# Gathers of the first two chunks with all fields of three examples, and their pair tiles picked by TensorE

## The chip, the cores and the metric

The kernel runs on one core of one Trainium2 chip. The metric is the device time in microseconds (us) of the whole program; lower is better. Before the change three runs took 1071.68, 1075.14 and 1076.42 us, median 1075.14. One further execution was recorded by the hardware profiler; all rows of the trace come from it. TensorE multiplies matrices, VectorE, ScalarE and GpSimd work on tiles in SBUF (on chip) and in PSUM (eight banks of 128 x 512 float32, where TensorE writes), and SyncE only starts transfers.

## What is computed

A compressed interaction network over 39 embedding fields of 16 elements, for 512 examples, and a small network behind it:

```python
e = jnp.stack([tbl_0[ids[:, 0]], ..., tbl_38[ids[:, 38]]], axis=1)     # (512, 39, 16): x
...
for k in range(3):                                                     # 128 units each
    z = jnp.einsum('bmd,bhd->bdmh', x, prev).reshape(b, D, m * h)
    t = jnp.einsum('bdc,co->bdo', z, ws[k]) + bs[k]
    t = jnp.transpose(t, (0, 2, 1))
    t = t / jnp.sqrt(jnp.sum(t * t, axis=(-2, -1), keepdims=True))
    logit.append(t)
    prev = t
# the sums over d of the three t, and dense_ctx: 400 features into layers of 512, 256 and 1
```

In layer 0 prev is x itself, so its products are pairs of fields; in layers 1 and 2 they are 39 fields by 128 units. All in float32.

## The kernel before

The batch is cut into 16 chunks of 32 examples. A chunk has 32 x 16 = 512 columns (example, element).

**From tables to pairs.** For each chunk GpSimd gathers rows by ten indirect DMAs (`gather`, L390), the 39 x 32 rows of field and example, 128 at a time and 96 in the last. SyncE stores them to `x_scratch` in device memory (`store_chunk`, L467 to L471) and loads them back with fields on partitions (`load_reps`, `load_partners`, helper L333): the field itself, repeated three times over 117 partitions plus 11 extra rows (`x_reps`), and its partners 2 to 19 fields on, in six tiles (`x_rot`). VectorE multiplies both (`make_pairs`, L896) into `z0`, in groups of two tiles that wait for `pairs_loaded[0]`, `[1]`, `[2]`; ScalarE makes the squares (`square_x`), VectorE their low part (L880). TensorE sums tiles 0 to 5 with folded weights (`pair_matmul`, L754, float32) and the squares (L752) into `acc0`: layer 0 before bias and norm. For chunk 0 three of the tiles aren't loaded but picked by TensorE out of 39 rows (`pick`, L771).

**Jobs.** Layers 1 and 2 are done in 128 jobs of 128 columns: `JOBS` has jobs 0 to 3 for layer 1 of chunk 0, then in turns four of layer 1 of a chunk and four of layer 2 of the one before. A job computes, for each field, weights times prev into a bank of four fields, by three float32r matmuls of split operands (`three_terms`, L686 to L688). Ten banks: five for ScalarE (`bank_a`, a ring of two), five for VectorE (`bank_d`, a ring of three), in turns D, A, D, A (places 0 to 9). ScalarE scales its banks by x (L531), GpSimd adds them (L407); VectorE scales and adds its 20 fields (u = 0 to 19) one by one (`add_field`, L918). ScalarE's banks are made seven ahead (`LEAD`), so before job 0 there are seven of them. `turn_sums` (L727) transposes the sum of job n - 1 at place 5 of job n.

**What sets the order.** Each engine's program is one list in a fixed order, with waits on semaphores; nothing is reordered. Tables of numbers say at which (job, place) or (job, field) other work stands in it: `PAIRS_AT` for VectorE's `make_pairs` of chunk c, `PAIR_MATMULS_AT` for the sums, `W2_HIGH_AT` and `W2_LOW_AT` for the split of layer 2's weights, `FINISHES` and `NORMS` for bias, sums and norm. In GpSimd's program `gather(it + 2, ...)` stands behind the adds a = 1, 2, ... of a job of round it. GpSimd's adds in job n's turn belong to bank 5n + 7 + a.

**The start.** GpSimd gathers chunks 0 and 1 and seven of chunk 2's ten before its first add. TensorE waits for chunk 0's gathers and keeps busy with matmuls whose results nobody reads (`keep_busy`, L777). ScalarE rounds the weights of layer 1 (`split_high`), VectorE takes the rest (`split_low`, L870). Chunk 1's pairs are made by VectorE before job 0 and summed by TensorE inside job 0.

Of the kernel before, what the change touches and what calls it, by code (L numbers as in the profile page):

```python
# [5 lines left out]
FIELDS = 39  # L6
# [107 lines left out]
for _c in range(1, CHUNKS):  # L114
    _it = _c - 1
    if _it == 0:

        _made = []
        _summed = {(0, 0): [0, 1], (0, 2): [2, 3], (0, 4): [4, 5], (0, 6): [6]}
    else:  # L120
        _first = (step_at(_it, 0), 2) if _it == 1 else (step_at(_it - 1, 7), 12)
        _made = [_first, (step_at(_it, 0), 12), (step_at(_it, 1), 12 if _it > 1 else 17), (step_at(_it, 2), 5)]
# [3 lines left out]
    if _it:  # L126
        SQUARES_AT[step_at(_it, 1), 3] = _c
# [10 lines left out]
GATHERS_BEFORE = 7  # L138
# [18 lines left out]
def cin_kernel(nc, idx_in, base_in, table, ctx_t, w0a, w0b, w1, w2, b0, b1, b2,  # L157
# [7 lines left out]
    with ExitStack() as ctx:  # L165
# [8 lines left out]

        ids_sb = sb("ids_sb", [128, CHUNKS * GATHERS], i32)
# [39 lines left out]
        twice = scaled[0:FIELDS, 0, 0, 0:2 * FIELDS]  # L215
        turns = scaled[0:FIELDS, 1, 0:PICKED, :]
# [32 lines left out]

        ids_loaded = sem("ids_loaded")  # L250
# [57 lines left out]

        NOT_LOADED = [PER_TILE + 2, 1, 0, 0]
# [68 lines left out]
        def _(pool):  # L378
# [4 lines left out]
            def start_chunk(c):  # L383
                if c >= 2:
# [756 lines left out]
```

## Time and profile before

| | |
|---|---|
| runs, us | 1071.68, 1075.14, 1076.42 (median 1075.14) |
| profiled execution | 1074.81 us, its span in the trace 1073.1 us |
| TensorE matmul | 1039.9 us busy, 97% of the span |
| VectorE | 970.8 us, 90% |
| GpSimd | 864.2 us, 81% |
| ScalarE | 797.3 us, 74% |
| chain that ended last | TensorE 66%, GpSimd 18%, VectorE 8%, issue 5% |

PE is TensorE's matmul unit, PEld its weight load, DVE is VectorE, ACT ScalarE, POOL GpSimd, SP SyncE; a q behind a name is that engine's sequencer, which issues DMAs. Times count from the span's start. A float32 matmul is recorded twice, so x12 in a row of L777 or L754 is six instructions; a float32r matmul once. The busy time of a matmul is modelled with its end, so the distance between starts is the better price. "idle before" is the engine's idle time ahead of an instruction, with what ended it.

### The profile page before, as it was taken

To read this page: it belongs to the slowest core of one execution; us is meant where nothing else is said; L and a number is where in the kernel's file an instruction comes from. 1 tells how busy PE (TensorE), PEld (TensorE's weight loads), DVE (VectorE), ACT (ScalarE), POOL (GpSimd) and SP (SyncE) were. 2 spreads that over 40 slices of the span, in tenths; PEclk is the share of its full clock that TensorE was granted. 3 is DMA by queue.
4 is the path that set the end of the run, shared out by engine and by line. 5 is a ranking of instruction groups with operands and counts; after the bars stand their busy time and mean duration, and the time that the engine had idled before them with its cause. 6 is when DMAs were issued, how large, how long until landed. Compare 5 with 4: busy or idle time off the path is not lost.

```text
span 1073.1 us, 18076 instructions
## 1 busy us (share of the span) xinstructions
PE 1039.9 (97%) x4386; PEld 790.4 (74%) x4386; DVE 970.8 (90%) x3326; ACT 797.3 (74%) x2670; POOL 864.2 (81%) x729
## 2 busy tenths in 40 slices
PE   2999999999999999999999999999999999999998
PEld 0466777878777787877778787777878777788783
DVE  2489999999999999999999999999999999999893
ACT  3476777868788786878778787877878787788772
POOL 6677888988888898888889888888988888586670
PEclk9999999999999999999999999999999999999999
DMA  5531030301403030120303012030301203000000
GB/s 189 140 100 23 3 83 3 84 2 16 125 3 82 3 83 2 28 58 3 83 3 83 1 34 52 3 83 3 84 2 24 61 3 82 1 1 1 1 1 1
DMA packets 59381, 44.02 MB, mean 41 GB/s; under 512 B 39177, under 2 KB 42121, under 8 KB 59146
## 3 DMA queue, kind: packets, MB, share of 16 engines
q1 hardware_dynamic: 51975, 36.49, 13.8%
q0 software_dynamic: 5120, 1.29, 1.4%
q10 hardware_dynamic: 2179, 5.07, 1.4%
q8 instruction: 35, 0.57, 0.2%
q14 instruction: 72, 0.59, 0.2%
HBM read 40.89 MB, written 1.94 MB: 40 GB/s over the span
## 4 chain that ended last, share of the span: by engine, by line
PE 66%; POOL 18%; DVE 8%; issue 5%; ACT 3%; DMA 1%; POOLq 0%; SPq 0%; DVEq 0%; ACTq 0%
POOL sums L407 13%; PE bank_a L686 10%; PE bank_d L686 9%; PE bank_d L688 9%; PE bank_d L687 9%; PE bank_a L688 9%; PE bank_a L687 9%; PE acc L754 7%; POOL gathered L390 4%; DVE sums L918 4%; ACT scaled L531 1%; PE turned L777 1%; ACT sums L531 1%; PE turned L727 1%; PE bank_d L855 1%
## 5 line engine op out<-in xcount | busy, mean ns | idle before, releaser
L407 POOL TENSOR_TENSOR sums<-sums,scaled 128x512 f32<-128x512 f32 (+1 forms) x512 | 648.1, 1267 | 146.0 <-ACT scaled L531 109.4
L918 DVE SCALAR_TENSOR_TENSOR sums<-bank_d,x_col,sums 128x128 f32<-128x128 f32 x2304 | 656.9, 343 | 50.8 <-PE bank_d L688 40.7
L531 ACT ACTIVATE scaled<-bank_a,x_col 128x128 f32<-128x128 f32 x1920 | 549.0, 383 | 131.5 <-PE bank_a L688 122.9
L686 PE MATMUL bank_d<-w_hi,prev_lo 128*128 128x512 f32 x640 | 284.4, 444 | 1.5 <-DVE sums L937 1.2
L686 PE MATMUL bank_a<-w_hi,prev_lo 128*128 128x512 f32 (+1 forms) x640 | 269.0, 420 | 4.8 <-POOL prev_lo L412 1.9
L688 PE MATMUL bank_d<-w_hi,prev_hi 128*128 128x512 f32 x640 | 252.6, 395 | 0.0
L687 PE MATMUL bank_d<-w_lo,prev_hi 128*128 128x512 f32 x640 | 252.6, 395 | 0.0
L688 PE MATMUL bank_a<-w_hi,prev_hi 128*128 128x512 f32 (+1 forms) x640 | 245.7, 384 | 0.0
L687 PE MATMUL bank_a<-w_lo,prev_hi 128*128 128x512 f32 (+1 forms) x640 | 245.3, 383 | 0.0
L531 ACT ACTIVATE sums<-bank_a,x_col 128x128 f32<-128x128 f32 x512 | 146.3, 371 | 77.9 <-PE bank_a L688 77.9
L390 POOL DMA_INDIRECT gathered<-in_table,idx x160 | 173.1, 1082 | 28.4 <-issue 17.5
L686 PEld LDWEIGHTS bank_a<-w_hi,prev_lo 128*128 128x128 f32 x640 | 120.5, 188 | 55.8 <-ACT scaled L531 14.8
L686 PEld LDWEIGHTS bank_d<-w_hi,prev_lo 128*128 128x128 f32 x640 | 120.8, 189 | 41.8 <-DVE sums L918 8.9
L687 PEld LDWEIGHTS bank_a<-w_lo,prev_hi 128*128 128x128 f32 x640 | 120.8, 189 | 34.7 <-issue 10.8
L687 PEld LDWEIGHTS bank_d<-w_lo,prev_hi 128*128 128x128 f32 x640 | 121.4, 190 | 29.1 <-issue 10.3
L688 PEld LDWEIGHTS bank_d<-w_hi,prev_hi 128*128 128x128 f32 x640 | 120.7, 189 | 28.5
L688 PEld LDWEIGHTS bank_a<-w_hi,prev_hi 128*128 128x128 f32 x640 | 120.4, 188 | 22.6
L754 PE MATMUL acc<-z,w_sb 128*128 128x512 f32 (+1 forms) x192 | 98.8, 604 | 0.5 <-DVE z L896 0.5
L896 DVE TENSOR_TENSOR z<-x_pairs 128x1024 f32<-128x1024 f32 (+1 forms) x46 | 86.9, 1888 | 3.3 <-DMA x_pairs<-x_scratch 3.3
L918 DVE SCALAR_TENSOR_TENSOR bank_d<-bank_d,x_col,sums 128x128 f32<-128x128 f32 x256 | 79.4, 351 | 0.0
L937 DVE TENSOR_TENSOR sums<-bank_d,sums 128x128 f32<-128x128 f32 x256 | 72.1, 282 | 0.0
L754 PEld LDWEIGHTS acc<-z,w_sb 128*128 128x128 f32 (+1 forms) x192 | 35.5, 192 | 12.9 <-issue 5.6
(83 smaller groups left out, 542.9 us busy)
## 6 DMA issues: line engine op xcount, KB each, us to landing
x_pairs<-x_scratch SPq DMA_DIRECT2D x135, 156.0 KB
x_pairs<-x_scratch SPq DMA_DIRECT2D x96, 78.0 KB
gathered<-in_table,idx POOLq DMA_INDIRECT x160
x_pairs<-x_scratch SPq DMA_DIRECT2D x92, 22.0 KB
x_scratch<-gathered SPq DMA_DIRECT2D x16, 72.0 KB
w_raw<-in_w ACTq DMA_DIRECT2D x1, 1024.0 KB, 5.0
w_raw<-in_w ACTq DMA_DIRECT2D x1, 896.0 KB
w_raw<-in_w SPq DMA_DIRECT2D x1, 832.0 KB, 7.0
```

The costliest lines, as they stand in the source:

```text
L390: nc.gpsimd.indirect_dma_start(out=gathered[0:n, c % 2, j, :], out_offset=None, in_=table[:, :], in_offset=bass.IndirectOffsetOnAxis(ap=id ...
L407: nc.gpsimd.tensor_tensor(out=sums[:, n % SUMS, 0:w, :], in0=sums[:, n % SUMS, 0:w, :], in1=scaled[:, a - 1, 0:w, :], op=ALU.add).then_inc ...
L531: op = nc.scalar.activation(to[:, i, :], bank_a[at % A_RING][:, i * UNITS:(i + 1) * UNITS], ACT.Copy, scale=x_of(c, q, a * PER_BANK + i))
L686: nc.tensor.matmul(to, lo, w_h, start=True, stop=False)
L687: nc.tensor.matmul(to, hi, w_l, start=False, stop=False)
L688: return nc.tensor.matmul(to, hi, w_h, start=False, stop=True)
L727: nc.tensor.transpose(turned[:, q * COLS:(q + 1) * COLS], sums[:, n % SUMS, TOTAL, :], identity[:, :]).then_inc(turn_done, 1)
L754: nc.tensor.matmul(acc0[:, :], w0_sb[0:rows, tile, :], z0[0:rows, tile, :], start=(tile == 0), stop=False)
L777: nc.tensor.matmul(turned[:, :], ones[:, :], w_raw[1][:, 0:4, :].rearrange("p m u -> p (m u)"), start=True, stop=True)
L896: nc.vector.tensor_tensor(out=z0[0:rows, tiles[0]:tiles[0] + count, :], in0=x_reps[min(p, 1)][0:rows, :].unsqueeze(1).to_broadcast([rows, ...
L918: nc.vector.scalar_tensor_tensor(out=taken(n, u) if u in LEFT else total, in0=taken(n, u), scalar=x_of(c, q, A_FIELDS + u), in1=total, op0 ...
L937: nc.vector.tensor_tensor(out=out, in0=in0, in1=in1, op=ALU.add).then_inc(merged, 1)
```

## The change

Chunks 0 and 1 no longer go through `x_scratch`. For each, eleven indirect DMAs gather all 39 fields of three examples at a time, 117 rows into the tile `direct` (`gather_direct`). They are worked on in three batches (`BATCHES`), of 192, 192 and 128 columns. VectorE sets the three examples of a gather apart (`apart_batch`: times 0 or 1, so that each example has columns of its own). TensorE picks from them, with matrices of zeros and ones (`turns`), both repeated tiles and all six partner tiles (`pick(c, b)`, eight float32 matmuls). ScalarE copies the two repeated ones (`make_reps`) and squares the first, VectorE multiplies the six others straight out of PSUM (`multiply_batch`), TensorE sums them (`sum_pairs`). The eight banks of a pick take turns over free PSUM banks, so a later item waits until an earlier one is used up. `turns` is built by VectorE now.

GpSimd issues the 22 gathers of chunks 0 and 1 before its first add and all ten of chunk 2 behind adds: seven in jobs 0 to 3 and three in jobs 4 and 5 (`GATHER_STEPS` and the tuple in its loop), chunk 3's in jobs 5 to 10. All of layer 2's weights are loaded by SyncE behind chunk 0's gathers, and all six pieces are split inside jobs. Chunk 1's picks and sums stand between the seven first banks (`LEAD_PICKS`, `LEAD_SUMS`), chunk 2's products in jobs 5 and 6.

```diff
-        _summed = {(0, 0): [0, 1], (0, 2): [2, 3], (0, 4): [4, 5], (0, 6): [6]}
+    if _c < DIRECT:
+        continue
+    if _it == 1:
+        _made = [(step_at(_it, 1), 6), (step_at(_it, 1), 12), (step_at(_it, 1), 17), (step_at(_it, 2), 5)]
+        _summed = {(step_at(_it, 1), 5): [0], (step_at(_it, 1), 8): [1], (step_at(_it, 2), 0): [2],
+                   (step_at(_it, 2), 2): [3], (step_at(_it, 2), 4): [4], (step_at(_it, 2), 6): [5],
+                   (step_at(_it, 2), 8): [6]}
     else:
...
-        _made = [_first, (step_at(_it, 0), 12), (step_at(_it, 1), 12 if _it > 1 else 17), (step_at(_it, 2), 5)]
+        _first = (step_at(_it, 0), 2) if _it == 2 else (step_at(_it - 1, 7), 12)
+        _made = [_first, (step_at(_it, 0), 12), (step_at(_it, 1), 12), (step_at(_it, 2), 5)]
...
-W2_LOADS_FIRST, W2_FIRST = 1, 2
-W2_LOW_BETWEEN = {0: 0, 2: 1}
-W2_HIGH_AT = {(1, 1): 2, (1, 2): 3, (2, 1): 4, (2, 2): 5}
-W2_LOW_AT = {(1, 14): 2, (2, 10): 3, (3, 10): 4, (4, 8): 5}
+GATHER_STEPS = [(0, 2), (1, 2), (2, 2), (3, 1)]
+W2_HIGH_AT = {(0, 4): 0, (1, 1): 1, (1, 2): 2, (1, 3): 3, (2, 1): 4, (2, 2): 5}
+W2_LOW_AT = {(1, 4): 0, (1, 14): 1, (2, 6): 2, (2, 14): 3, (3, 10): 4, (4, 8): 5}
+LEAD_PICKS = {1: 1, 4: 2}
+LEAD_SUMS = {1: 0, 3: 1, 6: 2}
...
+            for c in range(DIRECT):
+                for s in range(DIRECT_GATHERS):
+                    gather_direct(c, s)
             pool.wait_ge(ids_loaded, 32)
...
+            gathers_at = {}
+            left = [(c, j) for c in range(DIRECT, CHUNKS) for j in range(GATHERS)]
+            for n in range(NJ):
+                k, c, q = JOBS[n]
+                it, place = (c, q) if k == 1 else (c + 1, q + TILES)
+                count = dict(GATHER_STEPS).get(n, 0) if it == 0 else 2 if it > 1 else (2, 2, 2, 2, 2, 2, 1, 0)[place]
+                for a in range(1, 1 + count):
+                    if left and left[0][0] <= it + 2:
+                        gathers_at.setdefault((n, a), []).append(left.pop(0))
+            assert not left
             for at in range(LEAD):
                 add_bank(at)
             for n in range(NJ):
-                k, c, q = JOBS[n]
-                it, place = (c, q) if k == 1 else (c + 1, q + TILES)
...
-                    if 1 <= a <= per_step and first + a - 1 < GATHERS:
-                        gather(it + 2, first + a - 1)
+                    for c, j in gathers_at.get((n, a), []):
+                        if j == 0:
+                            start_chunk(c)
+                        gather(c, j)
...
+            sp.wait_ge(direct_gathered[0][NB - 1], 16 * (BATCHES[-1][1] - BATCHES[-1][0]))
+            for part in range(len(W_LOADS[2])):
+                load_raw(sp, 2, part)
+            store_chunk(DIRECT)
+            for c in range(DIRECT, CHUNKS):
+                sp.wait_ge(scratch_stored, (c - DIRECT + 1) * 48)
+                sp.wait_ge(*pairs_by(c - 1))
+                sp.wait_ge(x_turn_done, c)
                 for p in range(NP - 1):
                     if p < 2:
                         load_reps(sp, c, p)
-                    if c:
...
-                load_partners(act, 0, p)
+            for b in range(NB):
+                split_high(1, b)
+                make_reps(0, b)
+                square_x(0, b)
             act.wait_ge(bias_loaded, 48)
             copy_x(0)
-            square_x(0)
             finish(0, 0)
             roots(0)
             high(1, 0)
+            make_reps(1, 0)
+            square_x(1, 0)
             for at in range(LEAD):
                 scale_bank(at)
-                if at == LEAD - 2:
-                    square_x(1)
+                if at in LEAD_PICKS:
...
+            def pick(c, b):
+                columns = batch_columns(b)
+                x = apart[:, c, :, :, :].rearrange("p s b e -> p (s b e)")
+                pe.wait_ge(set_apart, c * NB + b + 1)
+                for item in range(PICKS):
+                    since = b * PICKS + item - len(pick_banks(c))
+                    if since >= 0:
+                        pe.wait_ge(*pick_taken(c, since // PICKS, since % PICKS))
+                    rows = 128 if item < 2 else tile_rows(item - 2)
+                    nc.tensor.matmul(pick_bank(c, b, item)[0:rows, columns], turns[:, item, 0:rows], x[:, columns],
+                                     start=True, stop=True).then_inc(picked, 1)
+            def sum_pairs(c, b):
...
-                pick(tile)
-            turn_x(0)
+            pe.wait_ge(turns_made, 2 * PICKS - 2)
+            pick(0, 0)
             pe.wait_ge(w0_folded, 1)
             pe.wait_ge(w0s_made, 1)
-            for tile in range(PAIR_TILES + 1):
-                pair_matmul(0, tile)
+            sum_pairs(0, 0)
+            pick(0, 1)
+            sum_pairs(0, 1)
+            pick(0, 2)
+            turn_x(0)
+            sum_pairs(0, 2)
             keep_busy(2)
             norms(0)
-            keep_busy(4)
+            pick(1, 0)
             for at in range(LEAD):
                 bank_for_act(at)
+                if at in LEAD_SUMS:
+                    sum_pairs(1, LEAD_SUMS[at])
+                if at in LEAD_PICKS:
+                    pick(1, LEAD_PICKS[at])
...
+            def multiply_batch(c, b):
+                columns = batch_columns(b)
+                if c:
+                    dve.wait_ge(pairs_summed, c)
+                for tile in range(PAIR_TILES):
+                    dve.wait_ge(picked, (c * NB + b) * PICKS + tile + 3)
+                    if tile % 2 == 0 and tile < 4:
+                        dve.wait_ge(reps_made, (c * NB + b) * 2 + tile // 2 + 1)
+                    rows = tile_rows(tile)
+                    nc.vector.tensor_tensor(out=z0[0:rows, tile, columns],
+                                            in0=pick_bank(c, b, tile + 2)[0:rows, columns],
+                                            in1=x_reps[min(tile // 2, 1)][0:rows, columns],
+                                            op=ALU.mult).then_inc(multiplied, 1)
+                low_squares(c, b).then_inc(multiplied, 1)
...
-                make_pairs(0, p)
+            for b in range(NB):
+                apart_batch(0, b)
+                multiply_batch(0, b)
+            split_low(1, 0)
             sum_values(0, 0)
             sum_squares(0, 0)
...
+            multiply_batch(1, 0)
+            split_low(1, 1)
+            apart_batch(1, 1)
+            multiply_batch(1, 1)
+            split_low(1, 2)
+            apart_batch(1, 2)
+            multiply_batch(1, 2)
```

**GpSimd, chunk 2's last gathers.** First the program before, in job 0's turn; `gathered` with 96 rows is a chunk's last gather, `sums` an add of a bank (its a_scaled is what ScalarE gives):

```order
L407 TENSOR_TENSOR sums<-sums,scaled 128x512 [waits a_added,a_scaled] x2
L390 DMA gathered<-in_table,idx 128x16
L407 TENSOR_TENSOR sums<-sums,scaled 128x384 [waits a_added,a_scaled]
L390 DMA gathered<-in_table,idx 128x16
L390 DMA gathered<-in_table,idx 96x16
L407 TENSOR_TENSOR sums<-sums,scaled 128x512 [waits a_scaled]
```

Now, the turns of jobs 4 (from its second add) and 5:

```order
L477 TENSOR_TENSOR sums<-sums,scaled 128x512 [waits a_added,a_scaled] x2
L460 DMA gathered<-in_table,idx 128x16
L477 TENSOR_TENSOR sums<-sums,scaled 128x384 [waits a_added,a_scaled]
L460 DMA gathered<-in_table,idx 128x16
L477 TENSOR_TENSOR sums<-sums,scaled 128x512 [waits a_scaled]
L477 TENSOR_TENSOR sums<-sums,scaled 128x512 [waits a_added,a_scaled] x2
L460 DMA gathered<-in_table,idx 96x16
```

The 96-row gather of chunk 2 has moved from job 0's turn to job 5's, behind seven gathers in jobs 0 to 3 and two in job 4.

**VectorE, chunk 2's first product.** Before, in job 4 (the memset and the add behind it are its field 0):

```order
L1022 MEMSET w1_raw 96x1024 [waits w1_lo_made]
L918 SCALAR_TENSOR_TENSOR sums<-bank_d2,x_col,sums 128x128 [waits a_added,d_ready]
L937 TENSOR_TENSOR sums<-bank_d1,sums 128x128 [waits merged,d_added]
L918 SCALAR_TENSOR_TENSOR sums<-bank_d2,x_col,sums 128x128 [waits a_added] x2
L896 TENSOR_TENSOR z0<-x_pairs 128x1024 [waits pairs_summed,pairs_loaded0]
L918 SCALAR_TENSOR_TENSOR sums<-bank_d2,x_col,sums 128x128 [waits a_added]
```

Now, in job 5 (the first row is its fields 4 to 6 with the one behind; in between stand the rows of the norm):

```order
L1029 SCALAR_TENSOR_TENSOR sums<-bank_d2,x_col,sums 128x128 [waits d_added,d_ready]
L1029 SCALAR_TENSOR_TENSOR sums<-bank_d2,x_col,sums 128x128 [waits d_added] x2
L1007 TENSOR_TENSOR z0<-x_pairs 128x1024 [waits pairs_summed,pairs_loaded0]
L1029 SCALAR_TENSOR_TENSOR sums<-bank_d2,x_col,sums 128x128 [waits d_added]
L1029 SCALAR_TENSOR_TENSOR sums<-bank_d0,x_col,sums 128x128 [waits d_added,d_ready]
```

The product has moved from field 2 of job 4 to field 6 of job 5, with the adds of its bank and the next queued behind it.

**TensorE, from chunk 0's norm to the first bank.** Before:

```order
L777 MATMUL turned<-w1_raw,ones 128x512 x2
L765 MATMUL small<-ssq,ones 128x32 [waits x_col_made,squares_summed]
L777 MATMUL turned<-w1_raw,ones 128x512 x4
L686 MATMUL bank_a0<-w1_hi,prev1_lo 128x512 [waits prev1_lo_made,w1_lo_made]
```

Now, where `h` holds the examples set apart and `sums` the picking matrices:

```order
L864 MATMUL bank_a0<-w1_raw,ones 128x512 x2
L840 MATMUL small<-ssq,ones 128x32 [waits x_col_made,squares_summed]
L854 MATMUL bank_d0<-h,sums 128x192 [waits set_apart]
L854 MATMUL bank_d1<-h,sums 128x192
L854 MATMUL bank_d2<-h,sums 128x192
L854 MATMUL turned<-h,sums 128x192
L854 MATMUL bank_d0<-h,sums 128x192 [waits reps_made]
L854 MATMUL bank_d1<-h,sums 128x192 [waits reps_made]
L854 MATMUL bank_d2<-h,sums 117x192 [waits multiplied]
L854 MATMUL turned<-h,sums 117x192 [waits multiplied]
L753 MATMUL bank_a0<-w1_hi,prev1_lo 128x512 [waits prev1_lo_made,w1_lo_made]
```

Eight picks of chunk 1 stand where four keep-busy matmuls did, the last four of them with waits on ScalarE and VectorE.

## Rows read from the trace of the kernel before

**Rows 1.** The page: busy time, share of the span and instructions of each engine.

```profile
PE 1039.9 (97%) x4386; PEld 790.4 (74%) x4386; DVE 970.8 (90%) x3326; ACT 797.3 (74%) x2670; POOL 864.2 (81%) x729
```

**Rows 2.** Stretches: from:to, length, busy per engine, granted clock, DMA share, GB/s.

```profile
80.00:100.00 20.00, 18.81 (x78) 13.83 (x77) 19.84 (x59) 14.38 (x48) 16.54 (x12) 1.00 0.16 36
...
200.00:400.00 200.00, 199.52 (x864) 155.24 (x864) 191.69 (x671) 156.81 (x533) 173.45 (x145) 1.00 0.22 53
```

**Rows 3.** The chain of waits, 0 to 80 us: start, duration, what.

```profile
18.41 2.29 DMA gathered<-in_table,idx
20.84 7.79 PE turned L777 x12
...
42.01 3.52 PE turned L777 x8
45.66 0.47 PE bank_a L686
```

**Rows 4.** In order of time, 0 to 60 us: start, duration, engine, line, what.

```profile
5.76 2.00 ACTq L362 DMA_DIRECT2D w_raw<-in_w  x4
...
8.43 0.94 POOL L390 DMA_INDIRECT gathered<-in_table,idx  x1 [0.30 <-issue]
...
38.71 0.80 PE L752 MATMUL acc<-z0s,w0s 117*128 117x512 f32 x1
...
52.73 0.40 PE L686 MATMUL bank_d<-w_hi,prev_lo 128*128 128x512 f32 x1
```

**Rows 5.** The page: a DMA issue with its size and time to landing.

```profile
w_raw<-in_w ACTq DMA_DIRECT2D x1, 1024.0 KB, 5.0
```

**Rows 6.** Groups by form, 20 to 46 us: count, busy, mean ns.

```profile
L892 DVE TENSOR_TENSOR z<-bank_d,x_pairs 128x512 f32<-128x512 f32 x3 | 2.1, 692 | 4.5 <-PE bank_d L771 4.2 <-issue 0.2
...
L765 PEld LDWEIGHTS small<-ssq,ones 128*128 128x128 f32 x2 | 0.3, 188 | 1.2 <-DVE ssq L945 1.2
```

**Rows 7.** Groups by form, whole span: low part of seven fields' weights.

```profile
L870 DVE TENSOR_TENSOR w_lo<-w_raw,w_hi 128x896 fp32r<-128x896 f32 x3 | 4.8, 1584 | 0.0
```

**Rows 8.** VectorE in order of time, 58 to 140 us.

```profile
58.31 3.18 DVE L918 SCALAR_TENSOR_TENSOR sums<-bank_d,x_col,sums 128x128 f32<-128x128 f32 x12
...
93.19 1.44 DVE L896 TENSOR_TENSOR z<-x_pairs 128x1024 f32<-128x1024 f32 x1
...
103.75 1.11 DVE L918 SCALAR_TENSOR_TENSOR sums<-bank_d,x_col,sums 128x128 f32<-128x128 f32 x4
```

**Rows 9.** TensorE in order of time: the first turn of sums (job 1).

```profile
71.51 0.27 PE L727 MATMUL turned<-identity,sums 128*128 128x128 f32 x1
```

**Rows 10.** The chain of waits, 80 to 140 us: behind place 4 of job 6.

```profile
114.14 0.86 PE acc L754 x2
```

**Rows 11.** GpSimd in order of time: gathers behind the first adds of jobs 4, 5, 8, 12.

```profile
95.90 0.97 POOL L390 DMA_INDIRECT gathered<-in_table,idx  x1 [0.15 <-POOL sums L407]
...
105.84 0.96 POOL L390 DMA_INDIRECT gathered<-in_table,idx  x1
...
132.41 0.96 POOL L390 DMA_INDIRECT gathered<-in_table,idx  x1 [0.15 <-POOL sums L407]
...
160.21 0.97 POOL L390 DMA_INDIRECT gathered<-in_table,idx  x1
```

**Rows 12.** SyncE in order of time: loads of chunk 1, store and loads of chunk 2.

```profile
39.95 9.49 SPq L333 DMA_DIRECT2D x_pairs<-x_scratch  x21
...
68.36 0.38 SPq L467 DMA_DIRECT2D x_scratch<-gathered  x1
...
71.74 8.44 SPq L333 DMA_DIRECT2D x_pairs<-x_scratch  x21
```

**Rows 13.** VectorE in order of time: chunk 1's first product.

```profile
47.02 1.23 DVE L896 TENSOR_TENSOR z<-x_pairs 128x1024 f32<-128x1024 f32 x1 [0.41 <-DMA x_pairs<-x_scratch]
```

**Rows 14.** Stretches, as rows 2: two of the start.

```profile
33.00:34.00 1.00, 1.00 (x3) 0.48 (x2) 1.00 (x2) 0.78 (x2) 0.70 (x2) 0.50 0.01 1
...
46.00:49.00 3.00, 2.29 (x10) 1.30 (x8) 1.84 (x2) 2.28 (x9) 0.12 (x1) 1.00 0.74 196
```

More of the change, by code:

```diff
@@ L33, with batch_columns, tile_rows @@
 NP = len(PAIR_GROUPS)
-PICKED = 3
+DIRECT = 2
+EXAMPLES = 128 // FIELDS
+DIRECT_GATHERS = -(-CB // EXAMPLES)
+BATCHES = [(0, 4), (4, 8), (8, DIRECT_GATHERS)]
+NB = len(BATCHES)
+PICKS = PAIR_TILES + 2
 SCRATCH_FIELDS = FIELDS + 5 * SLOT_FIELDS
 DMA_SCRATCH = 4096
+def batch_columns(b):
+    first, last = BATCHES[b]
+    return slice(first * EXAMPLES * EMB, min(last * EXAMPLES * EMB, ROWS))
+def tile_rows(tile):
+    return 128 if tile <= EXTRA_PAIRS[-1][0] + 1 else PAIR_ROWS
 PER_BANK = 4
@@ L383, in start_chunk, with gather_direct @@
             def start_chunk(c):
-                if c >= 2:
-                    pool.wait_ge(scratch_stored, (c - 1) * 48)
-                pool.wait_ge(idx_made, c + 1)
+                if c >= DIRECT + 2:
+                    pool.wait_ge(scratch_stored, (c - DIRECT - 1) * 48)
+                pool.wait_ge(idx_made, c - DIRECT + 1)
+            def gather_direct(c, s):
+                b = [first <= s < last for first, last in BATCHES].index(True)
+                at = c * DIRECT_GATHERS + s
+                nc.gpsimd.indirect_dma_start(
+                    out=direct[:, c, s, :], out_offset=None, in_=table[:, :],
+                    in_offset=bass.IndirectOffsetOnAxis(ap=first_idx[0:PAIR_ROWS, at:at + 1], axis=0)
+                ).then_inc(direct_gathered[c][b], 16)
             def gather(c, j):
@@ L484, in _ @@
                         load_reps(sp, c, p)
-                    if c:
-                        load_partners(sp, c, p)
-                if c == 1:
-                    for part in range(W2_LOADS_FIRST, len(W_LOADS[2])):
-                        load_raw(sp, 2, part)
+                    load_partners(sp, c, p)
                 if c + 1 < CHUNKS:
@@ L591, in _ @@
                 load_raw(act, 1, part)
-            for part in range(W2_LOADS_FIRST):
-                load_raw(act, 2, part)
             act.dma_start(top3_sb[:, :], w_top3).then_inc(top_bias_loaded, 16)
@@ L767, in norms @@
                                  start=True, stop=True).then_inc(norm_done, 1)
-            def pick(tile):
-                nc.tensor.matmul(bank_d[tile][:, :], turns[:, tile, :], x_rep[0:FIELDS, :],
-                                 start=True, stop=True).then_inc(picked, 1)
+            def pick(c, b):
[10 more added lines that the diff above has]
+            def sum_pairs(c, b):
+                for tile in range(PAIR_TILES + 1):
+                    pair_matmul(c, tile, b)
             def keep_busy(count):
                 for _ in range(count):
-                    nc.tensor.matmul(turned[:, :], ones[:, :], w_raw[1][:, 0:4, :].rearrange("p m u -> p (m u)"),
+                    nc.tensor.matmul(bank_a[0][:, :], ones[:, :], w_raw[1][:, 0:4, :].rearrange("p m u -> p (m u)"),
                                      start=True, stop=True)
@@ L1116 @@
     arrays = {
+        "first": direct_slots(np.asarray(inputs["ids"]), starts),
         "ids": slots(np.asarray(inputs["ids"])),
```

244 lines of the change are left out of this document (137 added, 107 removed).

## The prediction

> **What bounds the kernel now.** I read the busy shares first, then the busy time by stretches, the chain of waits through the first 80 us, the instructions in order of time around the stages that the change touches, and last SyncE's DMA issues. The shares and stretches show TensorE busy for 97% of the span and for 199.5 of every 200 us once the jobs run [rows 1, 2]: what keeps it idle at one point is not won back later. In the first 100 us it is otherwise. Until 20.84 TensorE does nothing; the chain runs through index load, ten gathers and the landing of the last (2.29 us from its issue), then keep-busy matmuls, picks, pair sums and norm, and the first bank matmul starts at 45.66 [rows 3]. From 58.31, where VectorE begins its adds [rows 8], to about 100 the chain is VectorE's; it is busy for 19.84 of the 20 us behind 80 [rows 2].
>
> I write (5, 6) for field 6 of job 5 on VectorE. A job has 30 bank matmuls, 27 at 0.23 and 3 of 384 columns at 0.17: 6.8 us.
>
> **The start.** Removed: store and load of chunks 0 and 1. Added: 22 gathers that land in place of 20, and in each chunk 24 picks, 18 float32 pair sums of 192 or 128 columns and 3 sums of squares, where chunk 0 had 3 picks and each chunk 7 wide sums. The index table is the first DMA instead of the second, so the first gather is issued near 6.5; one gather and its gap take 1.24 [rows 4]. The fourth lands at 6.5 + 1.4 + 2 x 1.24 + 2.3 = 12.7, and this isn't what TensorE waits for: its three keep-busy matmuls start when w1's first piece lands, 5.0 us behind an issue that moves from 5.76 to 6.2 [rows 4, 5], at 11.2. A float32 matmul is two records. At half clock one takes 0.86 us: 12 of them, half warm, took 7.79, where 8 warm ones took 3.52, 0.44 each [rows 3]. Six make 5.2 us, so the picks begin at 16.4. Batches 1 and 2 land at 17.7 and 21.4, before their turns.
>
> No row shows a 192-column float32 matmul. From below it is 192/512 of 0.86, 0.32 us (0.22 for 128 columns); from above half the wide one, 0.43. A weight load of 128 columns takes 188 ns [rows 6], and there are two, so I take 0.38 for either width. The Trainium skill ("TensorE: Matmul & The Clock Gate", LDWEIGHTS) puts a load at the columns over 1.2, 107 ns; by it the loads would hide and the lower bound would hold, 84 x 0.09 = 7 us less for both chunks. The trace disagrees with its 188 ns, and the measurement decides.
>
> A batch is 14 x 0.38 + 0.2 = 5.5 us. VectorE's six products (0.69 for 512 columns [rows 6], some 0.35 for 192) and ScalarE's four operations lie beside it. Three batches and the turn of x end at 16.4 + 16.5 + 0.4 = 33.3, where before the sum of squares ends at 39.5 [rows 4]: 6 us earlier. Bias, norm, root and prev take 6.1 as before; w1's first low part, 2.3 us, fits between VectorE's last product and the bias result. But all of pick(1, 0) stands ahead of the first bank, and its last two items wait for products that VectorE makes behind prev_lo: +1.3. First bank at 40.8, 4.9 earlier. Ahead of job 0 TensorE then has seven banks (6 x 0.70 + 0.52 = 4.7), 34 picks and sums at 0.38 (12.9) and 0.6 for squares: job 0 starts at 59.0. Before it starts at 52.73 [rows 4], with 5.4 us of chunk 1's sums still inside it. VectorE begins its adds at 59.7 instead of 58.31, and waits less for sums in job 0. With job 0 and the turn of x (7.3), the norm behind VectorE's last reduction, and six places of job 1 I come to the first turn of sums near 71.4; before it stands at 71.51 [rows 9]. So the start is worth 0: what the round trip gives back, the narrow matmuls take. Ends: 84 x 0.05 either way, -5 to +4.
>
> **Jobs 1 to 4.** Two more low parts of w2 (1.1 us as their size goes, 1.58 mean in the trace [rows 7]) move to where VectorE is the chain: +2.3. Two products of chunk 2, 1.44 us the first [rows 8], leave job 4: -2.6. VectorE is at (5, 6) near 104.3 (before: inside the row at 103.75 [rows 8]). ScalarE gets two high parts and GpSimd seven gathers more there; both idle for a fifth of the time or more, so 0, at most +1.
>
> **Chunk 2 decides.** Before, its rows were on their way from 71.74 [rows 12], and the product was made at 93.19 [rows 8]. Now its 96-row gather stands in GpSimd's program in the slot behind the second add of job 5's turn, and the product that needs it at (5, 6). The slot's time is known: it is the issue at 105.84 [rows 11], while VectorE was at (5, 6) at 104.6. In the new program no pair sums slow TensorE in jobs 4 and 5. The bank is finished about 1.4 us behind VectorE's (4, 15), which frees its ring buffer; the gather follows 2.8 later (scale 1.15, add 1.3, hand-overs); VectorE needs 4.8 from (4, 15) to (5, 6). That puts the gather at 103.7 to 104.2, within a microsecond of the wait that needs its data.
>
> Between them lie, all in the trace, 2.29 from issue to landing [rows 3], 3.4 for the store (68.36 to 71.74 [rows 12]), and nine loads at some 0.45 with the last landing 3.4 behind, 7.1 (39.95 to 47.02, where VectorE waited [rows 12, 13]): 12.8, or 12.4 with the shorter stores (3.0). The rows are there at 116.6, and VectorE stands at (5, 6) for 12.3 us. Queued behind it are all its adds, so the D banks; on TensorE the first sum of chunk 2, at place 5 of job 5, so everything. TensorE resumes at 116.6 + 1.25 = 117.85. To place 4 of job 6 it has nine banks (6.3) and five sums (4.3): 128.5. Before it is there at 114.14 [rows 10]. That is +14.4, the extra w2 parts and the moved products included.
>
> After 12 us without work TensorE will run at half clock: behind the first 20.84 idle, twelve records took 7.79 instead of 5.3 us, 2.5 lost [rows 3]. The rings hide part of it: +1.5, between 0 and 2.5. The Trainium skill ("TensorE: Matmul & The Clock Gate", "What's actually happening") holds that the throttled clock is the default and activity releases it; that rule would charge the full 2.5.
>
> **Chunk 3.** Its last gather moves from job 8 to the second slot of job 10, two jobs of 6.95 (132.41 to 160.21 are four [rows 11]) behind 132.41: 146.3. Data at 158.7. Its product, at (12, 2), is due 2.7 ahead of the slot of job 12 at 160.21 (as 93.19 to 95.90 [rows 8, 11]): 157.5. TensorE's sum at place 5 would come at 158.9 and gets its product at 160.0: +1.2, between 0 and 2. From chunk 4 on the order is as before.
>
> **Sum.** The profiled execution took 1074.81 us (span 1073.1, 1.7 around it); the median is 1075.14, the same within noise. 1074.8 + 0 + 14.4 + 1.5 + 1.2 = 1091.9; I say 1092. Its own range, with start -5 to +4, wait 11 to 16, clock 0 to 2.5 and chunk 3 0 to 2: 1083 to 1099.
>
> **Rivals.**
> A. The weight loads hide under the narrow matmuls, 0.32 and 0.22 for 0.38: 7 less on TensorE, of which VectorE's chain lets 5 through: 1087. Against it stands the 188 ns row; 8%. The skill's figure for a weight load speaks for it.
> B. TensorE stays at half clock in the start. For it: the granted clock is 0.50 in 33 to 34 us, behind a pause of 0.57 and picks of 39 rows [rows 14], and the new start has a pause of some 1.5 us inside pick(1, 0). Against: 46 to 49, with 0.7 of 3 us idle between full-height matmuls, kept 1.00 [rows 14]. Price: a narrow matmul at 0.70, on half of the 84 some 13 us, of which 8 beyond the waits: 1100. 11%.
> C. Chunk 2 is not waited for, because its rows come sooner or VectorE later than I read; the w2 parts stay: 1077, no change. It needs 12 us between gather and product, and [rows 11] gives them as 1 us apart in the wrong order. 10%.
> D. Faster: GpSimd's gather runs ahead of (5, 6) by 12.4 us or more, so the wait is hidden, and the 6 us won at the sum of squares reach job 0. That decides from a job 0 that starts before 54: 1074.8 - 6 = 1069. For it speaks only the earlier first bank. 5%.
> That the change doesn't do what it says I leave out: nothing in the program stores or loads chunks 0 and 1.
>
> **Numbers.** Forecast 66%. Within 0.5% (5.4 us, about what a measurement can tell here) is 1069.8 to 1080.5: faster 5% (D), same 9%, slower 86%. Range for 8 in 10: 1082 to 1101.
>
> **What would show it.** First bank matmul at 40 to 42, bank D of job 0 near 59, first turn of sums at 71 to 72; narrow float32 matmuls 0.38 apart; VectorE idle for 11 to 14 us between 104 and 117 with a DMA of x_pairs as releaser, TensorE idle beside it and at 0.50 behind it; a wait of 1 to 2 us near 172. I am wrong if the wait is under 5 us, or job 0 starts outside 54 to 64.

## The result

| kernel | median us | lowest to highest | runs | against before (95% interval) |
|---|---|---|---|---|
| before | 1074.2 | 1071.68 to 1076.42 | 4 | |
| changed | 1094.38 | 1093.18 to 1095.21 | 4 | 1.019 (1.0166 to 1.0214) |

The change costs 20 us. The profiled execution took 1093.18 us with a span of 1091.5, which is 18.4 above the 1073.1 of before; the traces are compared over these two spans.

The page of the changed kernel, TensorE's row and VectorE's products of pairs; it answers to [rows 1].

```profile
PE 1047.4 (96%) x4514; PEld 807.7 (74%) x4514; DVE 979.9 (90%) x3382; ACT 800.6 (73%) x2683; POOL 863.8 (79%) x730
...
L1007 DVE TENSOR_TENSOR z<-x_pairs 128x1024 f32<-128x1024 f32 (+1 forms) x42 | 83.7, 1994 | 16.9 <-DMA x_pairs<-x_scratch 16.9
```

VectorE stands for 16.9 us in front of x_pairs. Once the jobs run, nothing differs from [rows 2]: 199.49 of 200 us busy.

```profile
200.00:400.00 200.00, 199.49 (x867) 155.15 (x865) 191.60 (x663) 156.79 (x533) 173.21 (x144) 1.00 0.18 43
```

TensorE turns the sums of every job once, at place 5 of the next job. The starts of these turns in both traces, subtracted, show where time was won and lost (changed minus before, us):

| turn of job | 0 | 1 | 2 | 3 | 6 | 8 | 10 | 11 | 12 | 25 | last |
|---|---|---|---|---|---|---|---|---|---|---|---|
| changed | 64.37 | 72.77 | 81.28 | 89.44 | 134.43 | 148.68 | 165.18 | 172.10 | 186.64 | 286.97 | 1072.31 |
| shift | -7.1 | -6.1 | -5.1 | -4.7 | +11.4 | +11.4 | +13.7 | +13.7 | +17.9 | +17.9 | +18.4 |

So: the start wins 7.1; jobs 0 to 3 lose 2.4; chunk 2 loses 16.1; jobs 8 to 10 lose 2.3; chunk 3 loses 4.2; the rest 0.5. Sum +18.4.

**The start.** TensorE in order of time: keep-busy, sums of 192 columns and their sum of squares, three picks and the next, the same sums at 128 columns, the pause inside pick(1, 0), first bank, first D bank of job 0, first turn. It answers to [rows 3, 4, 9].

```profile
11.32 4.20 PE L864 MATMUL bank_a<-w_raw,ones 128*128 128x512 f32 x6 [11.32 <-DMA w_raw<-in_w]
...
17.95 2.12 PE L829 MATMUL acc<-z,w_sb 128*128 128x192 f32 x12
19.77 0.39 PE L825 MATMUL acc<-z0s,w0s 117*128 117x192 f32 x1
20.00 1.16 PE L854 MATMUL bank_d<-h,sums 117*128 117x192 f32 x6
21.00 0.49 PE L854 MATMUL turned<-h,sums 117*128 117x192 f32 x2
...
26.92 1.60 PE L829 MATMUL acc<-z,w_sb 128*128 128x128 f32 x12
28.28 0.31 PE L825 MATMUL acc<-z0s,w0s 117*128 117x128 f32 x1
...
34.15 1.49 PE L854 MATMUL bank_d<-h,sums 117*128 117x192 f32 x6 [1.63 <-ACT x_pairs L626]
...
35.66 0.53 PE L753 MATMUL bank_a<-w_hi,prev_lo 128*128 128x512 f32 x1
...
50.91 0.45 PE L753 MATMUL bank_d<-w_hi,prev_lo 128*128 128x512 f32 x1
...
64.37 0.27 PE L794 MATMUL turned<-identity,sums 128*128 128x128 f32 x1
```

Twelve records are six float32 matmuls; from one group's start to the next, six sums of 192 columns take 1.82 us, 0.30 each, three picks of 192 take 1.00, 0.33 each, and six sums of 128 take 1.36, 0.23 each. The first bank comes 10.0 us earlier than before, not 4.9, and bank D of job 0 starts at 50.91 instead of the 59.0 that I forecast. The lead of 7.1 us is that of one execution: in e3 and e4, whose start is the same, it was 6.1 and 6.2, and the three keep-busy matmuls took 5.46 us there instead of 4.20.

**Chunk 2.** Its last gather on GpSimd, then its store and loads on SyncE, then VectorE at (5, 6); they answer to [rows 8, 11, 12].

```profile
99.71 0.93 POOL L460 DMA_INDIRECT gathered<-in_table,idx  x1
```

```profile
101.99 0.38 SPq L542 DMA_DIRECT2D x_scratch<-gathered  x1
...
105.44 8.40 SPq L397 DMA_DIRECT2D x_pairs<-x_scratch  x21
```

```profile
111.66 1.22 DVE L1007 TENSOR_TENSOR z<-x_pairs 128x1024 f32<-128x1024 f32 x1 [13.97 <-DMA x_pairs<-x_scratch]
```

VectorE reached (5, 6) at 97.69 and the gather was issued 2.0 us behind that; from the gather to the product it is 11.95 us. The same stretch by windows (busy us of PE, PEld, DVE, ACT, POOL, then the granted clock, DMA share, GB/s): behind GpSimd's last operations only the DMA engines work, and TensorE's clock falls to the lower of its two levels, 0.50.

```profile
100.00:105.00 5.00, 0.00 (x0) 0.00 (x0) 0.00 (x0) 0.00 (x0) 2.61 (x3) 0.79 0.33 27
105.00:110.00 5.00, 0.00 (x0) 0.00 (x0) 0.00 (x0) 0.00 (x0) 0.00 (x0) 0.50 0.48 146
110.00:115.00 5.00, 1.97 (x3) 0.97 (x4) 2.89 (x9) 0.00 (x0) 0.00 (x0) 0.50 0.77 198
```

**Chunk 3.** VectorE waits again, and TensorE behind it; its first sum then takes 2.05 us, which is 1.02 at full clock.

```profile
172.97 1.73 DVE L1007 TENSOR_TENSOR z<-x_pairs 128x1024 f32<-128x1024 f32 x1 [2.88 <-DMA x_pairs<-x_scratch]
```

```profile
174.85 2.05 PE L829 MATMUL acc<-z,w_sb 128*128 128x512 f32 x2 [2.49 <-DVE z L1007]
```

```profile
176.00:178.00 2.00, 2.00 (x6) 1.21 (x5) 1.04 (x5) 0.00 (x0) 1.52 (x2) 0.51 0.74 199
```

### The profile page after: what moved, and what is told of

The parts are those of the page before. It is cut to its first block, busy times and chain, and to the rows that moved or that the text cites. A ratio compares the mean times of both kernels' runs of the same rounds, so it can differ in the third digit from the quotient of the medians.

```text
span 1091.5 us, 18380 instructions
## 1 busy us (share of the span) xinstructions
PE 1047.4 (96%) x4514; PEld 807.7 (74%) x4514; DVE 979.9 (90%) x3382; ACT 800.6 (73%) x2683; POOL 863.8 (79%) x730
## 4 chain that ended last, share of the span: by engine, by line
PE 64%; POOL 24%; issue 4%; ACT 3%; DMA 2%; DVE 2%; SPq 1%; POOLq 0%; ACTq 0%; DVEq 0%
POOL sums L477 19%; PE bank_a L753 9%; PE bank_d L753 9%; PE bank_d L755 8%; PE bank_d L754 8%; PE bank_a L755 8%; PE bank_a L754 8%; PE acc L829 8%; POOL gathered L460 4%; ACT sums L605 1%; ACT scaled L605 1%; PE turned L794 1%; PE bank_d L854 1%; PE bank_d L944 1%; DMA gathered<-in_table,idx 1%
## 5 line engine op out<-in xcount | busy, mean ns | idle before, releaser
L460 POOL DMA_INDIRECT gathered<-in_table,idx x140 | 153.6, 1097 | 21.6 <-issue 11.0
L754 PEld LDWEIGHTS bank_a<-w_lo,prev_hi 128*128 128x128 f32 x640 | 121.1, 189 | 34.7 <-issue 10.6
L829 PE MATMUL acc<-z,w_sb 128*128 128x512 f32 (+5 forms) x240 | 99.4, 516 | 16.7 <-DVE z L1007 16.7
L1007 DVE TENSOR_TENSOR z<-x_pairs 128x1024 f32<-128x1024 f32 (+1 forms) x42 | 83.7, 1994 | 16.9 <-DMA x_pairs<-x_scratch 16.9
L829 PEld LDWEIGHTS acc<-z,w_sb 128*128 128x128 f32 (+1 forms) x240 | 41.9, 191 | 24.1 <-issue 17.3
```

Of the source, the lines that this page charges most:

```text
L460: nc.gpsimd.indirect_dma_start(out=gathered[0:n, c % 2, j, :], out_offset=None, in_=table[:, :], in_offset=bass.IndirectOffsetOnAxis(ap=id ...
L754: nc.tensor.matmul(to, hi, w_l, start=False, stop=False)
L829: nc.tensor.matmul(acc0[:, columns], w0_sb[0:rows, tile, :], z0[0:rows, tile, columns], start=(tile == 0), stop=False)
L1007: nc.vector.tensor_tensor(out=z0[0:rows, tiles[0]:tiles[0] + count, :], in0=x_reps[min(p, 1)][0:rows, :].unsqueeze(1).to_broadcast([rows, ...
```

## The experiments

Medians are of runs beside the kernel before on the same chip; ratios carry their 95% interval.

**e1: chunk 2's gathers earlier.** Chunk 3's follow them in the same list, so they end in job 8 instead of job 10 too.

```diff
-GATHER_STEPS = [(0, 2), (1, 2), (2, 2), (3, 1)]
+GATHER_STEPS = [(0, 3), (1, 3), (2, 3), (3, 1)]
```

> The changed kernel with three of chunk 2's gathers in each of the jobs 0 to 2 of GpSimd's program and one in job 3, so that its ten end in job 3 instead of job 5 and chunk 3's end in job 8 instead of job 10; nothing else moves. My theory (what was lost is the two waits for x_pairs): both waits, 13.97 and 2.88 us on VectorE, and the half clock behind them vanish; what is left is the lead of the start, 7.1 us at the first turn of sums, less the 2.4 lost over jobs 1 to 4: turns of sums 4.7 us earlier than in the kernel before from job 3 on, time 1070 (1067 to 1073). Rival (the narrow matmuls and the two low parts of w2 cost what the gathers only hid): the waits go, but TensorE's own work keeps the time at 1076 or more.

Measured: 1073.99 us, ratio 1.0017 (1.0003 to 1.003). No product waits for x_pairs any more; taking the gathers forward gives back all but 0.2 of the 1.9%. But 1070 was missed: the first turn was 5.5 us early instead of 7.1, the shift of the turns went from -5.5 (job 0) to -1.0 (job 3), and from there to +1.0 (job 6). Jobs 1 to 2 by windows, changed kernel, e1 and before, one job each (POOL is the fifth busy figure):

```profile
72.77:81.28 8.51, 7.53 (x32) 5.45 (x31) 8.22 (x26) 6.36 (x21) 8.02 (x6) 1.00 0.02 3
```

```profile
74.57:83.93 9.36, 7.71 (x33) 5.43 (x31) 9.07 (x26) 6.32 (x21) 8.44 (x7) 1.00 0.02 3
```

```profile
78.83:86.41 7.58, 7.31 (x33) 5.54 (x32) 7.58 (x25) 6.51 (x21) 6.16 (x5) 1.00 0.49 117
```

With three gathers a job takes 9.36 us and GpSimd is busy for 8.44 of them, with none 7.58 and 6.16 (there with one low part of w2 instead of two). VectorE is busy for 9.07 of the 9.36 as well: its low part of seven fields took 1.97 us in e1's stretch and 1.08 in the changed kernel's. So these rows don't settle which of the two engines is the chain; e5 takes the gathers alone away. My step that gave these gathers a price of 0 to 1 us looked at GpSimd's idle share alone.

**e2: the kernel before, with only the late gathers, products and sums of chunks 2 and 3.**

```diff
-GATHERS_BEFORE = 7
+GATHER_STEPS = [(0, 2), (1, 2), (2, 2), (3, 1)]
...
+        _made = [(step_at(_it, 1), 6), (step_at(_it, 1), 12), (step_at(_it, 1), 17), (step_at(_it, 2), 5)]
```

> The kernel before with one part of the change alone: chunk 2's gathers, products and sums, and chunk 3's, at the places that they have in the changed kernel (last gather in job 5, product at (5, 6)); the start with its store and load, and w2's parts, as before. My theory: VectorE stops at (5, 6) for 12 to 14 us and near 170 for 2 to 3, each with TensorE at half clock behind it: 16 us at chunk 2 and 4 to 6 at chunk 3, so 1074.2 + 20 to 22 = 1095 (1090 to 1098). Rival (the late gathers are late only because the new start runs ahead or loads GpSimd): under 3 us of wait, 1077.

Measured: 1097.26 us, 1.0224 (1.02 to 1.0247). VectorE's two waits:

```profile
119.23 1.22 DVE L903 TENSOR_TENSOR z<-x_pairs 128x1024 f32<-128x1024 f32 x1 [14.22 <-DMA x_pairs<-x_scratch]
...
180.17 1.83 DVE L903 TENSOR_TENSOR z<-x_pairs 128x1024 f32<-128x1024 f32 x1 [2.80 <-DMA x_pairs<-x_scratch]
```

The waits need nothing of the new start; without its lead, the late gathers alone make the kernel slower than the whole change does (spans 1096.4 and 1091.5). Here w2's parts stay where they were, and the shift still grows by 1.3 us over jobs 0 to 3: I take that as the gathers' part of the changed kernel's 2.4.

**e3: TensorE kept at work through the wait.**

```diff
+                        if (c, tiles) == (2, [0]):
+                            pe.wait_ge(squared, FINISH_NO[0, 1] + 1)
+                            for _ in range(15):
+                                nc.tensor.matmul(acc0[:, :], ones[:, :],
+                                                 w_raw[1][:, 0:4, :].rearrange("p m u -> p (m u)"),
+                                                 start=True, stop=True)
```

> The changed kernel with 15 float32 matmuls of 512 columns (0.88 us each at full clock, 13.2 us in all) written into the accumulator ahead of chunk 2's first pair sum, where TensorE otherwise stands still for 14.24 us. The wait of VectorE stays. Theory: granted clock 1.00 right behind the wait; the half-clock stretch from 113.0 to 116.6 cost some 1.5 to 2 us, so 1092.4 to 1093. Rival (rings and VectorE hide the slow stretch): within 0.5 us of 1094.4.

Measured: 1089.51 us, 1.0154 (1.0133 to 1.0175). TensorE in order of time:

```profile
100.61 13.77 PE L924 MATMUL acc<-w_raw,ones 128*128 128x512 f32 x30
114.77 1.10 PE L829 MATMUL acc<-z,w_sb 128*128 128x512 f32 x2 [0.39 <-DVE z L1013]
```

The sum takes 1.10 us where it took 2.05. From chunk 2's product to the turn of job 6 it is 21.1 us (113.40 to 134.51) against 22.8 (111.66 to 134.43): the half clock cost 1.7 here. The median fell by more than I expected. Part of that is the kernel before, which took 1072.6 beside e3 and 1074.2 beside the changed kernel: by the ratios the gain is 3.9 us, by the spans 3.3. The rest is chunk 3, whose wait was shorter too in the profiled execution: its store began 2.3 us behind its last gather instead of 3.8, TensorE stood for 1.09 us instead of 2.49, and the clock stayed:

```profile
173.47 1.10 PE L829 MATMUL acc<-z,w_sb 128*128 128x512 f32 x2 [1.09 <-DVE z L1013]
```

The shift then grew by 1.3 us at chunk 3 instead of 4.2. That the landing was earlier by chance, and not by the edit, is my reading. e8 speaks for it: its edit lies in the start, its waits for chunk 2 are those of the changed kernel, and there too the store began 2.3 us behind the gather, TensorE stood for 1.09 us, the clock stayed and the shift grew by 1.3.

**e4: only chunk 3's gathers earlier** (gathers in each of jobs 4 to 11).

```diff
-(2, 2, 2, 2, 2, 2, 1, 0)[place]
+(2, 3, 3, 3, 2, 0, 0, 0)[place]
```

> The changed kernel with chunk 3's gathers alone moved up: three in each of GpSimd's jobs 5 to 7 and two in job 8, so that the tenth is issued about 14 us earlier; chunk 2's stay. Theory: the wait of 2.88 us near 170 and the half clock behind it vanish, 4.2 us by the turns of sums (shift to the kernel before 13.7 at job 11, 17.9 at job 12), and part of the 2.3 us that the shift grows by in jobs 9 and 10, where VectorE waits for GpSimd's sums: 1088 to 1090. Rival (chunk 3's product is late for another reason): 1094.

Measured: 1089.38 us, 1.0156 (1.0135 to 1.0177), as expected, though by the ratios it is only 3.7 us below the changed kernel. The second wait is gone, chunk 2's stays at 14.1. The shift at job 12 is 14.5 instead of 17.9.

**e5: nine of chunk 2's gathers in GpSimd's pauses.**

```diff
-GATHER_STEPS = [(0, 2), (1, 2), (2, 2), (3, 1)]
+GATHER_STEPS = [(0, 1)]
+LEAD_GATHERS = {0: 3, 1: 3, 5: 3}
```

> The changed kernel with nine of chunk 2's ten gathers in the stretches of the start in which GpSimd otherwise idles (three ahead of its second slot, three behind it, three behind the sixth) and one in job 0, so none is left in jobs 1 to 3; chunk 3's end in job 8. Theory now (what the early gathers of e1 saved in waits they took back because GpSimd is the chain in jobs 0 to 3: a job took 9.3 us with three gathers, 8.4 with two, 7.6 in the kernel before with none): a job takes 7.6 to 8.0 here, the lead of 7 us at the first turn shrinks by the 2.3 of w2's two low parts only, so 1069 to 1070. Rival (jobs 1 to 3 are longer because of VectorE's two low parts and an earlier start that TensorE can't follow, not because of gathers): as e1, 1074.

Measured: 1071.08 us, 0.9968 (0.9955 to 0.9981): 0.5% below e1 by the ratios, 2.9 us by the spans (1069.6 and 1072.5), and 0.3% faster than before. Jobs 1 to 3 took 8.40, 8.08 and 7.59 us, in e1 8.52, 9.36 and 9.23. w2's low parts stand in the same places in both, so the difference is the gathers'.

**e6: and three parts of w2 in the pauses of ScalarE and VectorE.** Their entries in the two tables go; the rows below are what stands in the start instead.

```diff
+            split_high(2, 0)
...
+                    split_high(2, LEAD_PICKS[at])
...
             apart_batch(1, 1)
+            split_low(2, 0)
             multiply_batch(1, 1)
...
             apart_batch(1, 2)
+            split_low(2, 1)
             multiply_batch(1, 2)
+            split_low(2, 2)
```

> e5 with w2's first three parts split in the start, where ScalarE and VectorE wait for the picks (high parts behind each batch of chunk 1's squares, low parts ahead of its last two products and behind them) in place of jobs 0 to 2. Theory: two low parts that VectorE no longer makes in its chain are worth 2.3 us against e5, the third one (in job 2 in e5) another 1.2: 3 less than e5, 1066 to 1067. Rival (the parts delay the products of chunk 1, and so the first D bank, by as much as they save): as e5.

Measured: 1067.85 us, 0.9944 (0.9925 to 0.9963), 3.2 below e5. In the profiled executions e6 is 2.9 us ahead of e5 at the first turn already, where e5 had the lower clock behind its pause and e6 did not (as in e9 below); over jobs 0 to 3 e6 then gains 1.8 where e5 loses 1.5, and that is what moving w2's parts is worth there. The same job as above now takes 6.93 us and TensorE is busy throughout:

```profile
70.88:77.81 6.93, 6.93 (x33) 5.68 (x32) 6.72 (x26) 6.58 (x22) 5.72 (x5) 1.00 0.39 90
```

**e7: e5 with chunk 2's products and sums back at their old places** (the tables of the kernel before).

> e5 with chunk 2's products back at (4, 2), (4, 12), (5, 17), (6, 5) and its pair sums in jobs 4 to 6, as in the kernel before. Theory: the data are there in time at either place, and TensorE and VectorE have the same work, so within 1 us of e5. Rival: VectorE's chain gets longer by 2.6 us in job 4, before TensorE takes over, and the time rises by as much.

Measured: 1071.53 us, 0.9971 (0.9955 to 0.9987): as e5. Where the products stand is worth nothing that the medians show. In the traces it is worth 1.0 us: e5's lead shrinks from 3.2 at the turn of job 3 to 2.2 at that of job 6, e7's is 5.5 at both.

**e8: 24 more narrow matmuls.**

```diff
             keep_busy(2)
+            for columns in [192] * 12 + [128] * 12:
+                nc.tensor.matmul(bank_a[0][:, 0:columns], ones[:, :], ...
```

> The changed kernel with 24 more narrow float32 matmuls ahead of the first norm: 12 of 192 columns, then 12 of 128, all with the full 128 rows and a weight load of 128 columns each, which measures their price by itself. By the prediction's 0.38 they take 9.1 us; if the two weight loads hide under the columns (0.33 and 0.22) they take 6.6. The first turn of sums then comes 6.6 us (or 9.1) behind the 64.4 of the changed kernel.

Measured, in a single run: 1096.92 us. TensorE:

```profile
31.46 6.74 PE L883 MATMUL bank_a<-w_raw,ones 128*128 128x192 f32 x48
38.04 0.31 PE L840 MATMUL small<-ssq,ones 128*128 128x32 f32 x2
```

From 31.46 to 38.04 it is 6.58 us: 12 x 0.33 + 12 x 0.22 = 6.6, where 0.38 makes 9.1. The row holds both widths. Two loads of 190 ns, as their records have them here, would make 0.38 a matmul, so the loads hide, and the length of a load's record is not what a load occupies. The Trainium skill ("TensorE: Matmul & The Clock Gate", LDWEIGHTS) gives 107 ns for such a load; two of them make 0.21, and 0.22 a matmul leaves room for that, though no row here shows a load's price by itself.

The first turn of sums comes 7.1 us later than in the changed kernel (71.48). Only 3.7 of them are left in the span, because chunk 3 cost 1.3 here instead of 4.2 and a pause near the end kept its clock, 1.6 (see below e10).

**e9 and e10: e6 with e7, and the pause inside pick(1, 0) filled.** e9 joins the edits of e6 and e7; e10 adds this ahead of the fifth pick's wait:

```diff
+                    if (c, b, item) == (1, 0, 4):
+                        for _ in range(3):
+                            nc.tensor.matmul(bank_a[0][:, 0:256], ones[:, :], ...
```

> e6 with chunk 2's products and sums at the places of the kernel before, as in e7. In e6 the lead over the kernel before grew to 9.4 us at the fourth turn of sums and was 7.85 from the seventh on; in e7 it was 5.5 at both. Theory: with the products back in job 4, VectorE's slack there is used and the lead stays above 8, so 1066 to 1067, and ahead of the kernel before by 7 to 9 us (ratio 0.992 to 0.994). Rival: TensorE has no slack left in jobs 4 to 6 either way, 1068 as e6.

Measured: 1067.82 us, 0.9927 (0.991 to 0.9943): e6's median. The ratio is 1.8 us below e6's, but within its interval. The step that I expected is there in the trace, since the shift is -6.5 at the turn of job 3 and -6.6 at that of job 6, where e6 went from -9.4 to -7.9; the start hid it. In its profiled execution the first turn came at 66.87, in e6's at 63.96. Of these 2.9 us, 1.4 stand at the norm already (31.66 and 30.28; the keep-busy group took 5.40 and 4.33), and 1.5 come behind TensorE's 1.63 us pause, where e9 had the lower clock; the 4 us in e9 and then in e6:

```profile
36.00:40.00 4.00, 4.00 (x14) 3.45 (x14) 4.00 (x9) 2.43 (x7) 1.79 (x2) 0.60 0.07 6
```

```profile
36.00:40.00 4.00, 4.00 (x26) 3.83 (x25) 3.24 (x4) 2.79 (x11) 3.68 (x3) 1.00 0.06 6
```

> e9 with three float32 matmuls of 256 columns (1.32 us by 0.44 each, half of a 512-column one) in TensorE's 1.63 us pause inside pick(1, 0). In the profiled executions of e1, e5 and e9 the granted clock was 0.55 to 0.60 in the 4 us behind that pause, in those of the changed kernel, e3, e4, e6, e7 and e8 it was 1.00 behind the same pause. Theory (my rival B, in some executions only, at 1.5 to 2.5 us): granted clock 1.00 from 33 to 41 us and a median 0.5 to 1 below e9's, 1067. Rival (the first turn of sums varies by 3 us for other reasons): median as e9, 1067.8, with the same spread.

> e9 once more, beside e10 on the same chip. If the clock behind the pause differs between executions, this one's profile may show either 1.00 or about 0.6 from 36 to 40 us; its median is 0.5 to 1 above e10's by the theory, equal by the rival.

Measured: e10 1066.33 us (1064.51 to 1067.12), 0.9927 (0.9912 to 0.9942); e9 again 1066.51 (1064.57 to 1069.27), 0.9931 (0.9914 to 0.9948). Both profiled executions kept 1.00. The medians don't differ, so whether the filler gains anything stays open; only e10's highest run is 2 us lower. The lead that I expected of e9 is there in both, 9.0 us from the turn of job 4 on. All three are 0.7% faster than the kernel before, the best here.

**A pause near the end that goes either way.** In all thirteen profiled executions TensorE pauses between the turns of jobs 121 and 122 for 1.85 to 1.88 us, because it waits for GpSimd; the kernel before and e9 again:

```profile
1014.78 0.50 PE L686 MATMUL bank_a<-w_hi,prev_lo 128*128 128x512 f32 x1 [1.88 <-POOL prev_lo L412]
```

```profile
1006.11 0.50 PE L753 MATMUL bank_a<-w_hi,prev_lo 128*128 128x512 f32 x1 [1.87 <-POOL prev_lo L476]
```

Behind it the granted clock was 0.50 from 1016 to 1018 us in the kernel before and 1.00 in e9 again. It fell in six of the thirteen (before, changed, e3, e4, e7, the first e9), and between the two turns these took 10.6 us where the others took 9.05. So 1.6 us of a difference between two spans can be this alone: +18.4 is free of it, since both kernels had it, but of the 19.0 between the spans of the changed kernel and e1 it is a part. The 53 runs of the kernel before that were made beside the experiments go the same way: the 7 with a mean clock of 1.00 took 1069.5 to 1072.7 us, the 23 with 0.995 took 1074.8 to 1076.5.

## Why the prediction came out right, and where it didn't

The kernel is slower, as forecast, and 1092 is 2.4 below the median. The cause that I named is shown: e2 has it without the rest, e1 takes it away and 1.7 of the 1.9% go with it, some 18.6 us. Rival C needed 12 us between gather and product; the trace has them 2.0 apart in the wrong order.

By its own signs the account of the start failed. I had called myself wrong if the wait was under 5 us or job 0 started outside 54 to 64. The wait was 13.97, but job 0 started at 50.91, the first bank at 35.66 and not between 40 and 42, the first turn came at 64.37 and not at 71 to 72, and the narrow matmuls are 0.22 to 0.33 apart and not 0.38.

So the number is good by errors that cancel. Up to the turn of job 6 I forecast 0 + 14.4 + 1.5 = 15.9 us and 11.4 were measured; behind it I forecast 1.2 and 7.0 were measured. By its terms:

- Start, 0 forecast, -7.1 measured. The mis-sized term is the narrow matmul: 0.38 forecast, 0.33 and 0.22 fit e8. 56 of 192 columns and 28 of 128 make 56 x 0.05 + 28 x 0.16 = 7.3 us. These were my lower bounds for one matmul and rival A's mechanism, to which I gave 8%, and I went above them on the length of one record. The end of -5 that I gave the start was too near besides, since 84 x 0.05 takes the margin of 192 columns for those of 128 too. Three smaller ones: the first gather was issued at 3.92, not 6.5, yet batch 0 was picked up at 14.18, not 12.7; the picks began at 15.35, not 16.4.
- Jobs 0 to 3: GpSimd's seven gathers were given 0, at most 1. They cost 1.3 (e2), and w2's parts the rest of the 2.4, to within some tenths: in e5, where w2's parts and one gather are left, the lead shrank by 1.5 over these jobs.
- Chunk 2: 12.3 us of wait forecast, 13.97 measured. The path itself was right (12.4 forecast, 11.95 measured from gather to product); the gather came 2 us behind VectorE instead of beside it. That GpSimd's longer jobs are the reason is likely and not shown. The whole term, 14.4 with w2's parts and the moved products, was 16.8 by the turns (2.4 + 16.1 - 1.7 of clock).
- Clock: 1.5 forecast, 1.7 measured (e3). My upper end of 2.5 came from the lengths of the first twelve records (7.79 us); the granted clock reads 1.00 beside them, so that they ran at the lower level is read from their lengths alone.
- Chunk 3: 1.2 forecast, 4.2 measured. The wait was 2.88, of which 1.5 are the later landing of its last gather (3.8 us instead of 2.3), and I charged no half clock for it. Behind 2.49 us without work TensorE had it, behind 1.09 (e3) not.
- Jobs 8 to 10, +2.3: not in the forecast. In the changed kernel VectorE waited for GpSimd's sums there, 1.50 us ahead of 154.57 and 1.67 ahead of 163.26. In e1, where chunk 3's gathers end in job 8, the shift stays at 1.0 from job 6 to job 12; but in e4, where they end in job 8 too, behind the wait for chunk 2, it grew by 1.5. That the gathers are behind it is likely, their share is open.

Had I sized the narrow matmul right and left the rest, I would have said 1087 (rival A), and been further off for a better reason. That the median came so near 1092 is luck; that it is some 20 us above before and not below is not. The upper end of my own range, 1099, leaves out the 2.1 us by which the term of chunk 2 is longer than its wait, and which the lower end has; with them it is 1101.

Rival B's mechanism is real, at a lower price: the 1.63 us pause was followed by a clock of 0.55 to 0.60 in the profiled executions of e1, e5 and the first e9, and by 1.00 in those of the changed kernel, e3, e4, e6, e7, e8 and the second e9. It cost 1.5 us (e9 against e6), not 8, since the clock came back after some 4 us.

Rival D's sign came, a job 0 before 54, and its gain was held off by the places of the gathers and of w2's parts: in e6 the lead is 7.6 us at the first turn and 7.9 at job 7.

## What to carry to other kernels

A change that frees one stage also decides when the next stage's data are asked for: write down each producer's issue slot beside its consumer's place, and compare them with the measured path between (here 12 us), before adding up what was saved. An engine that is idle for a fifth of the time isn't free: price work by the job in which it stands, and put it into pauses that the trace shows. A record's length isn't a price; take the distance from start to start of a run of such records, and if none exists, keep both bounds in the sum.

## What was new about the hardware

- A float32 matmul takes 0.30 to 0.33 us at 192 columns and 0.22 to 0.23 at 128 (24 of them in 6.58 us), though each of its two weight loads shows 190 ns.
- The same 1.6 us pause of TensorE halved the clock in three of ten profiled executions, a 1.9 us pause near the end in six of thirteen, for 1.6 us each time. A pause of 1.09 us kept it twice (e3, e8), one of 2.49 us lost it both times (changed kernel and e2), those of 13.5 to 14.5 too (changed kernel, e2, e4, e8).
- At half clock behind a 14 us wait the loss was only 1.7 us.
